# Attention in a fused layer: who masks the maxima pass, who turns the maxima, and how often the values are weighed

## The reference

```
q_lat, k_lat = rope(q @ q2l.T + b), rope(k @ kv2l.T + b)      # 4 sequences, 16 heads, T = 2048, latent 32
att = einsum('bhql,bhkl->bhqk', q_lat @ wqk.T + b, k_lat) * L ** -0.5
att = softmax(where(causal, att, -inf), axis=-1)
y   = einsum('bhqk,bhkl->bhql', att, v_lat) @ l2o.T + b
x   = layernorm(x + y @ cproj.T + b)
x   = layernorm(x + moe(x))                                     # 8 experts, top 2, capacity 1024
```

## Time and profile before

| | us |
|---|---|
| median of 3 runs (lowest, highest) | 3424.54 (3422.44, 3427.51) |
| the profiled execution: its span | 3474.8 |
| attention, first max unit to last matmul | 466 to 2450 of that span |
| one pass of the attention loop | 242.6 |

### The profile page before, as it was taken

How to read it: one execution, slowest core, us unless ns; L and a number is a source line. 1 busy time by engine, 2 the same in 40 slices (tenths; PEclk the granted TensorE clock), 3 DMA queues, 4 the chain that set the end, 5 groups by cost and what they waited for, 6 DMA issues and landing times. The chain is left out here.

```text
span 3474.8 us, 63180 instructions
## 1 busy us (share of the span) xinstructions
PE 3037.1 (87%) x17753; PEld 1989.2 (57%) x17753; DVE 2395.9 (69%) x4681; ACT 1917.3 (55%) x3710; POOL 794.3 (23%) x764
## 2 busy tenths in 40 slices
PE   7888869999999999999999999999699968999600
PEld 6677735555555555555555555555476648888500
DVE  7999977877877777777778778777355534434244
ACT  4666616666656666666566666566344435545322
POOL 6777810100100001000001000000144440000265
PEclk9999959999999999999999999999799989999855
DMA  6666653332322333233232323322722203221255
GB/s 220 213 234 217 221 144 70 70 70 47 91 63 55 71 70 70 47 85 76 49 70 70 71 47 92 69 52 67 261 104 93 81 18 111 94 68 58 69 166 170
DMA packets 252240, 348.83 MB, mean 100 GB/s; under 512 B 57906, under 2 KB 138139, under 8 KB 250656
## 3 DMA queue, kind: packets, MB, share of 16 engines
q1 hardware_dynamic: 237344, 313.59, 31.5%
q0 software_dynamic: 14592, 31.51, 3.4%
HBM read 206.54 MB, written 147.85 MB: 102 GB/s over the span
## 5 line engine op out<-in xcount | busy, mean ns | idle before, releaser
L765 DVE TENSOR_REDUCE att_partial_max<-att_max_bank 128x1 f32<-128x512 f32 (+2 forms) x2640 | 1450.5, 603 | 404.9 <-PE att_max_bank L613 304.3
L728 ACT ACTIVATE att_probs<-att_score_bank 128x512 f32<-128x512 f32 (+3 forms) x2560 | 1203.8, 536 | 746.0 <-PE att_score_bank L653 711.9
L653 PE MATMUL att_score_bank<-att_q_st,att_k_st 98*128 98x512 f32 (+3 forms) x2563 | 1031.5, 408 | 29.9 <-issue 29.9
L613 PE MATMUL att_max_bank<-att_k_st,att_q_st 96*128 96x512 f32 (+2 forms) x2640 | 990.1, 384 | 29.2 <-DVE att_ident_b L757 24.6
L653 PEld LDWEIGHTS att_score_bank<-att_q_st,att_k_st 98*128 98x128 f32 x2563 | 497.0, 194 | 499.2 <-ACT att_probs L728 353.8
L669 PE MATMUL att_acc_bank<-att_probs,att_v_st 128*32 128x512 f32 (+3 forms) x5120 | 606.3, 546 | 0.0
L613 PEld LDWEIGHTS att_max_bank<-att_k_st,att_q_st 96*128 96x128 f32 x2640 | 515.1, 196 | 138.9 <-DVE att_partial_max L765 47.7
L749 POOL TENSOR_SCALAR_AFFINE_SELECT att_probs<-att_probs 128x512 f32<-128x512 f32 x256 | 162.4, 634 | 1818.9 <-ACT att_probs L728 1818.9
L211 POOL TENSOR_TENSOR proj_op_low<-proj_turned,proj_op_high 128x512 fp32r<-128x512 f32 x192 | 274.8, 1463 | 58.6 <-ACT proj_op_high L340 58.2
L616 PE MATMUL att_max_bank<-att_mask,att_ident_b 128*128 128x128 bf16 x1066 | 252.5, 237 | 0.0
L616 PEld LDWEIGHTS att_max_bank<-att_mask,att_ident_b 128*128 128x128 bf16 x1066 | 106.6, 100 | 157.8 <-issue 115.8
(11 more groups left out here) (227 smaller groups left out, 3975.3 us busy)
## 6 DMA issues: line engine op xcount, KB each, us to landing
qk_parts<-proj_parts SPq DMA_DIRECT2D x64, 1024.0 KB, 4.5
att_q_st<-qk_parts SPq DMA_DIRECT2D x204, 256.0 KB, 3.9
att_k_st<-qk_parts SPq DMA_DIRECT2D x204, 256.0 KB, 5.8
att_v_st<-v_tokens SPq DMA_DIRECT2D x68, 256.0 KB, 6.7
v_tokens<-proj_v_tok SPq DMA_DIRECT2D x64, 256.0 KB, 4.5
exp_w<-in_ew SPq DMA_DIRECT2D x16, 1024.0 KB, 7.6
proj_xt<-in_x_t POOLq DMA_DIRECT2D x16, 512.0 KB, 4.7
y_heads<-att_y SPq DMA_DIRECT2D x64, 128.0 KB, 2.3
```

Source lines behind the costliest of these rows:

```text
L613: last = nc.tensor.matmul(out[:, 0:width], q_st[0:3 * L, c, j, t * P:(t + 1) * P], k_st[0:3 * L, par, kb, j, 0:width], start=True, stop=(k ...
L653: nc.tensor.matmul(score_ps[h % (HG * NK) % 3][:, q0:CH], k_st[:, p, kt // TT, j, (kt % TT) * P:(kt % TT + 1) * P], q_st[:, c, j, q0:CH], ...
L728: nc.scalar.activation(probs[:, k % 4, j, q0:CH], score_ps[(HG * k + j) % 3][:, q0:CH], ACT.Exp).then_inc(exped, 1)
L765: nc.vector.tensor_reduce(partial_max[:, m % 2, j * TT + t, kb:kb + 1], max_ps[max_bank(u)][:, 0:width], AX.X, ALU.max).then_inc(unit_redu ...
```

## The change

What it does, all in `attend`:

- The mask matmul goes. On a diagonal unit VectorE runs one `tensor_tensor_reduce` in place of the `tensor_reduce`: it adds the constant `edge` (128 x 512, zeros and then the triangle in its last 128 columns), writes the sum to a scratch tile and gives the maximum of it. The two bf16 casts before the loop go with the mask.
- The maxima are split before they are turned. VectorE copies and subtracts 128 x 16, and turns the 128 x 32 result in 32 x 32 blocks. These three instructions stand one slot apart behind `combine_max`. The turned maxima lie in 8 pieces, and SyncE writes them with 8 DMAs where it had 2. TensorE has no transpose of maxima any more.
- The bank `misc` is gone; there are two banks `acc`, used by turns, and the sums are turned within their own bank. ScalarE reads a chunk two steps later than it did.
- TensorE's list is now 320 slots of (one score, one max unit), scores 3 heads ahead. After every eighth slot it weighs two key steps in a row. The first burst of a pass stands after the 13th slot; the last one weighs four steps, and three slots follow it. Sums are turned five slots after their burst. SyncE's list follows the same slots.

```diff
-                if kb == c:
-                    last = nc.tensor.matmul(out[:, width - P:width], ident_b[:], mask[:], start=False, stop=True)
...
+                if kb < c:
+                    nc.vector.tensor_reduce(best, bank[:], AX.X, ALU.max).then_inc(unit_reduced, 1)
+                else:
+                    width = (t + 1) * P
+                    dve.sem_inc(masked_max_due, 1)
+                    nc.vector.tensor_tensor_reduce(
+                        out=edge_sum[:, u % 4, 0:width], in0=bank[:, 0:width], in1=edge[:, CH - width:CH], scale=1.0, scalar=LEAST,
+                        op0=ALU.add, op1=ALU.max, accum_out=best).then_inc(unit_reduced, 1)
...
+            def high_max(base, m):
+                nc.vector.tensor_copy(max_parts[:, m % 2, 0:HG * TT], neg_max[:, m % 2]).then_inc(max_split, 1)
+            def low_max(base, m):
+                nc.vector.tensor_tensor(max_parts[:, m % 2, HG * TT:ROWS], neg_max[:, m % 2],
+                                        max_parts[:, m % 2, 0:HG * TT].bitcast(F32), ALU.subtract).then_inc(max_split, 1)
+            def turn_max(base, m):
+                nc.vector.transpose(max_rows[:, m % 2], max_parts[:, m % 2].bitcast(F32)).then_inc(rows_ready, 1)
...
+            for part in range(2):
+                row = q_st[3 * L + part:3 * L + part + 1, m % NC].rearrange("w j (t n) -> w (j t) n", n=P)
+                for at in range(0, P, L):
+                    rows = slice(at + part * HG * TT, at + (part + 1) * HG * TT)
+                    sp.dma_start(row[:, :, at:at + L].bitcast(F32), max_rows[rows, m % 2]).then_inc(shift_in[m % 2], 16)
...
+                for i in range(NS):
+                    score(it, AHEAD + i)
+                    max_unit(it, LEAD + i)
+                    done = (AHEAD + i + 1) // BURST - 1
+                    if (AHEAD + i + 1) % BURST == 0 and done and AHEAD + i < NS:
+                        for k in range(PAIR * (done - 1), PAIR * done):
+                            weigh(it, k)
+                        if done == NK // PAIR - 1:
+                            for k in range(PAIR * done, PAIR * (done + 1)):
+                                weigh(it, k)
+                    n = sums_due_at(i)
+                    if n is not None:
+                        turn_sums(it, n)
+                turn_sums(it, 2 * NC - 1)
...
+                for i in range(NS):
+                    n = chunk_weighed_at(i)
+                    if n is not None:
+                        sp.wait_ge(weighted, it * NK + last_step(n))
                         load(sp, slot[n // NC + 1], (n // NC + 1) % 2, n % NC)
```

More of the change, by code:

```diff
@@ L441, with maxima_through @@
 MU_END = [HG * TT * (c + 1) * (c + 2) // 2 for c in range(NC)]
-def maxima_ending(k):
-    done = LEAD + PER_STEP * (k + 1)
-    group, rest = divmod(done, MUG)
+PAIR = 2
+AHEAD = 3
+TURN_AFTER = 5
+def maxima_through(units):
+    group, rest = divmod(units, MUG)
     if rest == 0:
@@ L466, in attend @@
         v_st = sb("v_st", [P, 2, NC, TT, HG * L])
[L467 to L470, removed]
+        probs = sb("probs", [P, 2 * PAIR, HG, CH])
+        edge = sb("edge", [P, CH])
+        edge_sum = sb("edge_sum", [P, 4, CH])
         ident = sb("ident", [P, P])
@@ L480, in attend @@
         max_ps = [ps(f"max{i}", [P, CH]) for i in range(3)]
-        acc = ps("acc", [P, CH])
-        misc = ps("misc", [P, CH])
+        acc = [ps(f"acc{i}", [P, CH]) for i in range(2)]
         consts_in = sem("consts_in")
-        mask_set = sem("mask_set")
+        edge_set = sem("edge_set")
         ones_set = sem("ones_set")
@@ L503, in attend @@
         y_out = [sem(f"y_out{i}") for i in range(2)]
-        for free in (y_done, max_split, *y_out):
+        nc.sync.sem_inc(y_done, 2)
+        for free in y_out:
             nc.sync.sem_inc(free, FREE)
         block = ctx.enter_context(nc.Block())
-        loads = [(mask_f[:], a["mask"]), (ident[:], a["ident"])]
         qk_src = d["qk"].rearrange("s c f (j p) n -> s c f p j n", p=L)
[L510 to L542, removed]
         def chunk_step(k):
@@ L549, in last_step, with burst_slot, chunk_weighed_at, sums_due_at @@
             return (n // NC) * KSG + CHUNK_END[n % NC]
+        def burst_slot(k):
+            return min(BURST * (k // PAIR + 2) - AHEAD, NS - AHEAD) - 1
+        def chunk_weighed_at(slot):
+            ends = [n for n in range(2 * NC) if burst_slot(last_step(n) - 1) == slot]
+            return ends[0] if ends else None
+        def sums_due_at(slot):
+            ends = [n for n in range(2 * NC - 1) if burst_slot(last_step(n) - 1) + TURN_AFTER == slot]
+            return ends[0] if ends else None
+        def maxima_at(slot):
+            return maxima_through(LEAD + slot + 1) if 0 <= slot < NS else None
         def load(sp, slot, par, c):
@@ L615, in max_unit @@
-                if kb == c:
-                    last = nc.tensor.matmul(out[:, width - P:width], ident_b[:], mask[:], start=False, stop=True)
-                last.then_inc(unit_scored, 1)
-            def misc_free(it, use):
-                before = [what for what, _ in uses[:max(use - MISC_HEAD, 0)]]
-                if use:
-                    pe.wait_ge(max_split, it * (2 * NC) + ((min(use, MISC_HEAD) + before.count("max")) + FREE))
-                if use >= MISC_HEAD:
-                    pe.wait_ge(y_done, it * (2 * NC) + (before.count("sum") + FREE))
@@ L754, in _ @@
         def _(dve):
[L755 to L757 removed]
+            dve.wait_ge(consts_in, 32)
             def reduce_unit(base, u):
@@ L1759, in const_arrays @@
         "fold8": ((row[:, None] % L) == np.arange(E)[None, :]).astype(f),
-        "mask": np.where(row[None, :] > row[:, None], NEG, 0.0).astype(f),
+        "edge": np.where(np.arange(CH)[None, :] - (CH - P) > row[:, None], NEG, 0.0).astype(f),
     }
```

219 lines of the change are left out of this document (90 added, 129 removed).

## The result

The changed kernel takes 3439.55 us (median of 20 runs, 3426.60 to 3451.76), the kernel before 3427.47 (20 runs, 3420.47 to 3443.16): ratio 1.0029, 95% interval 1.0018 to 1.0041. It is 12 us slower. The forecast was 34 us faster; the time lies in the forecast's range, on the other side of no change.

The account below looks back on a forecast made before the run. TensorE was taken to bound the attention loop, VectorE 20% behind. Per pass -28.7 + 22.0 + 2.9 + 0.3 = -3.5 us, -28 in eight; with -2.5 and -3 before and in the lead, -34, so 3390 us, range 3345 to 3455.

Parts of the forecast that it names:

- x: Extra VectorE time of a masked reduction over a plain one: taken as 0.10 us, between 0.08 and 0.13.
- (a): Max pass on TensorE: removing 128 mask matmuls a pass at 0.115 us each saves 14.7 us a pass.
- (b): TensorE's bursts: 80 become 39 a pass, each saving 0.26 us of transitions, -10.7 us a pass.
- (c, d, i): Per pass: eight maxima transposes off TensorE, -0.9 us; sums turned without a shared transition, +1.3; later `acc` reads, nothing.
- VectorE in long stretches, less today's waits: Max units waiting for reductions in longer stretches: +22.0 us a pass at x = 0.10; today's waits go, -2.2.
- (g): First max unit of slot 176 waits for chunk 3's load, which starts after a merged burst: +2.9 us a pass.
- (f): Opening of a pass on TensorE: less time lost to the low clock, -1.5 us a pass.
- (h): Scores of chunk 3 wait for shift rows, now eight DMA issues: +0.15 us each, +0.3 a pass.
- rival 3: The hole at slot 176 also drops TensorE's clock: up to 3.2 us a pass, 3415 us; chance 0.1.
- The table of stretches: TensorE's against VectorE's time in a pass's 39 stretches: +22.5 us at x = 0.10, +22.0 after corrections.
- rival 2: Masked reduction's write-out is hidden, x below 0.05: 6.5 us a pass more gain, 3340 to 3365 us; chance 0.2.
- Rival 1: VectorE's masked reduction is the new bound: slower from x = 0.155, 3445 us at x = 0.2; chance 0.27.

Follow-up runs that it names:

- e1: The kernel before with only the max pass's masks moved from TensorE matmuls into VectorE's reduction on diagonal units: 3374.0 us, ratio 0.9835.
- e5: The changed kernel with bursts of one key step and VectorE reducing only half of each unit's columns: 3367.4 us, ratio 0.9818.
- e3: The changed kernel with VectorE reducing only the first half of each unit's columns, TensorE's work unchanged: 3306.9 us, ratio 0.9638.
- e7: The changed kernel with bursts of one key step and shift rows moved by four DMAs for eight: 3349.1 us, ratio 0.9770.
- e2: The changed kernel with each next-slot load started when the chunk's last step is exponentiated, not weighed: 3398.1 us, ratio 0.9904.
- e10: The changed kernel, double bursts kept, with loads started at the exponential and shift rows moved by four DMAs: 3405.0 us, ratio 0.9918.
- e9: The changed kernel with plain reductions on the diagonal and no mask in the max pass: 3430.1 us, ratio 0.9989.
- e4: The changed kernel with bursts of one key step and four probabilities buffers kept: 3403.8 us, ratio 0.9926.

## Why the prediction was wrong

The measured account of a pass against the prediction's, us. The first column is the prediction with its own slope taken to x = 0; most measured sizes are differences of two rows of the table above.

| step | predicted | measured | from |
|---|---|---|---|
| (a) masks off TensorE | -14.7 | -7.8 | e1 against before, main steps (109 masks; nothing came of the rest) |
| (b) merged bursts | -10.7 | -10.8 | e5 and e3, 9.1 x 39 / 33 |
| (c, d, i) turned maxima, sums, reads | +0.4 | -0.7 | e7 against e1 |
| VectorE in long stretches, less today's waits | 15.5 - 2.2 | +11.9 | e3 (13.6), e7 against e5 (1.7) |
| (g) load of chunk 3, with its clock | +2.9 | +6.4 | e2 |
| (f) clock and turn of the pass | -1.5 | +1.5 | turn, changed against before |
| (h) shift rows | +0.3 | +0.5 | e3 and changed against e10 |

The first column adds up to -10.0. The second is +1.0, with 39 bursts counted; the main steps, which have 33 of them, are -5.2 in the table of runs, its three parts together +2.7, and the mean pass of the trace +2.5.

**(a) is the step that failed most.** "A 384 + 384 pair with a mask takes 0.48; without it 0.474 - 0.107 = 0.367. So 0.115 each, 128 a pass: -14.7." The price is near for a mask between two scores where nothing else waits (0.12 to 0.13). I multiplied it by all 128, without looking at where they stand: 58 stood at the end of a stretch, where the transition into the burst is paid anyway (0.067), and part of the others before a unit that waits in any case (mean 0.091). That makes 10.0 of the 14.7. The edit gave 7.8: of the 19 masks outside the main steps nothing was seen in the time (21.5 for 21.4, and a turn of 25.0 for 24.2), and a small part came back as waits for VectorE. 6.9 us a pass too much, 55 in all, more than the whole forecast gain of 34. With (a) at 7.8 the forecast, at its own x of 0.10, would have been some 3.4 a pass slower, +27 (less what the lead gives). That x was 0.01 took some 47 of it back (6.5 x 0.9 x 8), and (f) and (g) came on top. The lead gave 2.7 of its 5.5 (its last unit starts at 509.2 where it was 511.85).

**(g) was seen, and mis-sized.** The place, the cause and the hole's length were as predicted (2.9; measured 3.4). That the clock goes with it was rival 3, at 0.1, and its price of up to 3.2 a pass was right; e2 shows both together at 6.4 (5.8 by means). A 4 us hole with the low clock behind it stood in the earlier trace rows, and a hole of 3 was treated as unlikely to do the same.

**(f) had the wrong sign.** I had counted the low clock over the first slots only, and the count doesn't come out: 8.5 slots in the 6.3 us that the working leaves for them are 0.74 each, where a slot at 1.2 GHz takes 0.85 in the changed kernel. The turn of the pass is 1.5 longer (1.1 by means). Around it the trace has 7 to 17 us at 1.2 GHz, 12.6 in the mean, where before had 7 to 10, 7.8 in the mean; TensorE's idle time there is the same, some 4.5. VectorE's waits aren't the reason, for e3 has 10 to 14 us of low clock too, and e5, which differs from it only by single bursts, 6.8 in each pass, as e7 has. So it comes with the double bursts, but which part of them does it stays open: no run took the first slots without values, or the last burst of four steps, apart by itself.

**x and the table.** x is 0.01 (e9), not 0.10; the rows of plain add and reduction were the right neighbours, and the write-out's price, taken from the earlier trace rows, was wrong, since it is hidden beside the next reduction. The Trainium skill ("VectorE: DVE Perf Modes", section "Two Vector instructions with no wait between them") says that such an op is two instructions; the trace agrees, with 83 ns for the second. The prediction's estimate of x = 0.08, made from the Trainium skill's 75 ns per instruction ("Vector Engine (DVE) Microarchitecture Reference", section "5.2 Measured stream behaviour on trn2"), is not borne out for this second instruction: e9 gives 0.01 to 0.02. The half rate that the Trainium skill gives for two SBUF sources (the same page, section "7. Points that are easy to get wrong") doesn't occur here, with one source in PSUM: 680 ns against 685. The table of stretches itself was right: 13.1 predicted for the main steps, 13.6 measured by e3. So rival 2's premise held (x below 0.05) and its time, 3340 to 3365, did not, because (a), (f) and (g) gave back 13 us a pass. Rival 1's side came true without its mechanism. One sum in rival 1 is wrong as it stands: "+6.5 + 3 - 3.5" is 6.0; its 3445 belongs to 6.5 - 3.5 = 3.0.

**The signs that the prediction named.** Reduction under 750 ns: yes. Waits of max units for VectorE: 22 a pass said, 27.9 by the weight loads' rows. One hole of 2 to 3 us released by a load: yes, 3.4. Bursts of 1.8 us, 38 of two steps and one of four: yes, 1.85. VectorE's busy time below 205 a pass: yes, 181 (1269.7 / 7). All of them held, and the forecast failed: none of them tested (a). That the time lay inside the range was luck: some 107 us of error one way ((a), (f) and (g)) were in part made good by 47 the other way (x). Its sign would have been the masks' own price by place, which the trace of before could have shown, and TensorE's busy time in a pass: it fell by 4.0, low clock included, where (a), (b) and (c) together wanted 26.3.

## What to carry to other kernels

A small matmul's price is what follows it minus what would follow without it: price it at each place where it stands, before multiplying by the count. Merging bursts saves TensorE's transitions (0.28 each here) and takes from the engine beside it the pause in which it caught up; with three banks and a consumer at 0.60 per unit the second was larger (VectorE's waits went up by 11.9 us a pass against 10.8 saved), so the masks alone, with single bursts, were the better kernel. And the transfer that came 3.4 us late here cost 5.8 to 6.4, once the clock is counted.

## What the runs showed of the hardware that I had not expected

The two-input reduction with a maximum out of it (`tensor_tensor_reduce`, one source in PSUM, float32) runs at the plain reduction's speed, 680 ns for 512 columns, and its 83 ns read is hidden. TensorE's order has its own cost: where nothing else waits, the score behind a bf16 mask is followed by its max unit 0.08 to 0.09 late. TensorE's waits of 2.5 to 4.5 us in the changed kernel were each followed by 6.8 to 10.2 us at 1.2 GHz. The issue of a shift DMA takes nearly the same for 2 KB (5.02 for eight) and for 4 KB (2.64 for four in e7), so half the DMAs are half the time. A wait of 2.8 us a pass on shift rows in e4 was worth 55 us in eight passes when it went.
